# Eight matmuls of ones behind the transpose of the negated maxima, and key heads 376 elements apart

## The chip, the cores and the metric

One Trainium2 chip, one of its cores. The metric is the device time of one execution in microseconds (us), the median over several runs.

## What is computed

Two transformer layers on a batch of 8, with 112 tokens of width 256 per batch and a context of 375 tokens:

```python
x = x + L0_xcond(layernorm(x), ctx, ctx, tau, delta)   # 16 heads of 16, keys and values from ctx
x = x + L0_ffn(layernorm(x))                           # int8-like and ternary matmuls, conv of 3 taps, silu
x = x + L1_xcond(ctx, layernorm(x), len, pt)           # windowed attention
x = x + L1_ffn(layernorm(x))                           # 8 experts, one per token

# L0_xcond, the part that the change touches
scores = einsum('bhqd,bhkd->bhqk', q, k) * tau + delta
p_attn = softmax(scores / sqrt(DK), axis=-1)
x      = einsum('bhqk,bhkd->bhqd', p_attn, v)
```

## The kernel before

The work of the first three parts is a pipeline over the 8 batches. In one round of the loop at the end of the TensorE program, L874, the scores of one batch, the rest of the attention of the batch before, and the feed-forward and second attention of older batches are issued in an order written out by hand. The other engines have such loops too (SyncE, ScalarE, GpSimd, VectorE), and semaphores tie them together. A steady round takes some 31 us. After the rounds comes the expert layer.

Steps of the attention in `L0_xcond`, for batch b:

- `p_k`, `p_q`, `p_v` project keys, queries and values. Keys and queries are each split into three bf16 parts by ScalarE and GpSimd. SyncE writes the parts to DRAM (`p_kwrite` L475, `p_qwrite` L497) and reads them back (`p_kread` L478 to 489, `p_qread` L507) into the stacked tiles `kst` and `qst`. Partitions 0 to 95 of `kst` hold the parts of the keys in six bands of 16 partitions, 96 to 98 the bias `delta`, 99 to 101 ones. Each half of the heads (m = 0, 1) is read by three DMAs of 48, 32 and 16 partitions and a small one for `delta`.
- `a_scores(b, i)`, L694, computes two heads' scores, 112 queries by 375 keys. It reads `kst` as the moving operand, one head of even and one of odd number. VectorE takes the maxima (`a_max`, L1714), and `a_neg` negates them and splits them into three bf16 parts `nm`.
- TensorE's `a_max(b)`, L710, transposes `nm` into `pOb`. VectorE copies that to `nmT` (L1733), and ScalarE's queue issues three small DMAs (`a_stack`, L1179) that lay `nmT` into partitions 99 to 101 of `qst` and count up `nm_loaded`.
- `a_scoresT(b, n)`, L718, n = 0 to 11, computes the transposed scores, four heads and 125 keys at a time, with `kst` as the weights. The rows of `nmT` subtract the maximum. The result goes in turn to the two PSUM banks `pE[0]` and `pE[1]`, and ScalarE takes the exponential (`a_exp`, L1188, semaphore `exp_done`). `a_pv` multiplies with the values.

Between `a_max` and the first `a_scoresT` of a batch TensorE has `t_dg2` (L803, two records of a small fp32 matmul for the feed-forward; VectorE's `t_hq` L1611 scales with its result) and `p_v(i, 0)` (L653, whose result ScalarE copies to `vaug` before it goes on to the key split `p_km`). Behind the first two `a_scoresT` come `t_down` (L809), a third, `p_v(i, 1)`, a fourth, and `t_xqT` (L771), which waits for the quantized activations `xq` and the diagonal `dg` of VectorE (`t_xq`, L1614).

```python
def spin(n):
    for _ in range(n):
        mm(pS[:, 1, :], onesb[:, :], onesb[:, :].unsqueeze(1).to_broadcast([128, 4, 128]), True, True)
...
pe.wait_ge(ones_made, 1)
spin(8)
```

These eight matmuls of ones, 128x512 in bf16, stand at the start of TensorE's program already.

Of the kernel before, what the change touches and what calls it, by code (L numbers as in the profile page):

```python
# [5 lines left out]
def pixart_block(nc, A, out):  # L6
# [8 lines left out]
    B, T, D = A["x"].shape  # L15
    L = A["ctxT"].shape[3]
    NH, DK = 16, 16
    KT = 3
    LT = L // KT
    DC = D // 128  # L20
    HM = NH // DC
    HG = 4
    NG = NH // HG
    NP = NH // 2
    F0 = A["w1T"].shape[1] // DC
    M0 = F0 // 128
    NE, _, F1 = A["L1_ffn_W1"].shape
    M1 = F1 // 128
    FB = D
# [8 lines left out]
    KD = KS + 3  # L38
    KX = KD + 3
# [7 lines left out]
    with ctx:  # L47
        def sb(name, shape, dt=fp32):
            return ctx.enter_context(nc.sbuf_tensor(name, shape, dt))

        def sem(name):
            return ctx.enter_context(nc.semaphore(name))

        def dram(name, shape, dt=fp32):
            return nc.dram_tensor(name, shape, dt).ap()


        d_k = [dram(f"d_k{i}", [DC, 3, 128, L], bf16) for i in range(2)]
        d_q = [dram(f"d_q{i}", [DC, 3, 128, T], bf16) for i in range(2)]
        d_delta = dram("d_delta", [B, 3, L], bf16)  # L60
# [6 lines left out]

        EW = DC * F1 + M1 * D
        W = sb("W", [128, NE, EW])
# [4 lines left out]
        def carve(words):  # L74
            a = taken[0]
            taken[0] += words
            assert taken[0] <= (NE - 1) * EW
            return late[:, a:a + words]

        kst32 = [carve(NH * L // 2) for _ in range(2)]  # L80
        qst32 = [carve(NH * T // 2) for _ in range(2)]
        kst = [t.bitcast(bf16).rearrange("p (h l) -> p h l", h=NH) for t in kst32]
        qst = [t.bitcast(bf16).rearrange("p (h t) -> p h t", h=NH) for t in qst32]
        pexp = [carve(KT * HG * T).rearrange("p (k n) -> p k n", k=KT) for _ in range(2)]
        vaug = [carve(KT * NH * 32).rearrange("p (k h c) -> p k h c", k=KT, h=NH) for _ in range(2)]
        kf = carve(DC * L).rearrange("p (m l) -> p m l", m=DC)
        kr = carve(DC * L).rearrange("p (m l) -> p m l", m=DC)
# [37 lines left out]
        onesb = sb("onesb", [128, 128], bf16)  # L125
# [130 lines left out]
        pS = ps[:, 0:2, :]  # L256
        pE = [ps[:, 2, :], ps[:, 3, :]]
# [33 lines left out]
        exp_done = sem("exp_done")  # L291
# [19 lines left out]
        kst_loaded = [sem(f"kst_loaded{i}") for i in range(4)]  # L311
# [18 lines left out]
        ones_loaded = sem("ones_loaded")  # L330
# [103 lines left out]
        def _(sp):  # L434
# [42 lines left out]
            @batch  # L477
            def p_kread(b, m):  # L478

                sp.wait_ge(k_written[m], 16 * (b + 1))  # L480
                if b == 0:
                    sp.wait_ge(delta_written, 16)
                if b >= 2:
                    sp.wait_ge(st_ps, 12 * (b - 2) + 6 * (m + 1))
                src = d_k[b % 2][m].rearrange("t (d h) l -> (t d) (h l)", h=HM)
                dst = kst[b % 2][:, HM * m:HM * m + HM, :]
                for lo, n in ((0, 3), (48, 2), (80, 1)):
                    sp.dma_start(dst[lo:lo + 16 * n].rearrange("p h l -> p (h l)"), src[0:16 * n]).then_inc(kst_loaded[2 * m + b % 2], 16)
                sp.dma_start(dst[KS:KD], d_delta[b].unsqueeze(1).to_broadcast([3, HM, L])).then_inc(kst_loaded[2 * m + b % 2], 16)

            @batch
# [7 lines left out]
            @batch  # L499
            def p_qread(b):  # L500

                sp.wait_ge(q_written, 16 * (b + 1))
                if b >= 2:
                    sp.wait_ge(st_ps, 12 * (b - 1))
                src = d_q[b % 2].rearrange("m t (d h) l -> (t d) m (h l)", h=HM)
                for r, (tq, _) in enumerate(TERMS):
                    sp.dma_start(qst[b % 2][16 * r:16 * r + 16].rearrange("p (m h) l -> p m (h l)", m=DC),  # L507
                                 src[16 * tq:16 * tq + 16]).then_inc(qst_loaded[b % 2], 16)
# [36 lines left out]
            sp.dma_start(prepi[:, 0:1], A["_lenS2"].unsqueeze(1)).then_inc(len_loaded, 16)  # L545
            for i in range(2):
                sp.dma_start(qst32[i][KS:KD], A["ones"][:, 0:NH * T // 2]).then_inc(ones_loaded, 16)
                sp.dma_start(kst32[i][KD:KX], A["ones"][:, 0:NH * L // 2]).then_inc(ones_loaded, 16)
            sp.dma_start(ebn, A["L1_ffn_b2"]).then_inc(eb_loaded, 16)
            load_rows(1)  # L550
            load_ctx(1)
            for i in range(B + 5):
                w_delta(i - 2)
                w_win(i - 1)
                p_kwrite(i - 2, 0)
                p_ge(i - 2)
                w_tab(i - 2)
                p_qwrite(i - 2)
                p_kread(i - 2, 0)
                p_qread(i - 2)  # L560
                p_kwrite(i - 2, 1)
                p_ctx(i)
                p_kread(i - 2, 1)
                p_rows(i)
                w_eb(i - 5)
# [12 lines left out]
        def _(pe):  # L578
            def mm(o, l, r, start, stop):
                return pe.matmul(o, lhsT=l, rhs=r, start=start, stop=stop, skip_group_check=True)  # L580

            def tr(o, i, ident):
                n = i.shape[0]
                return pe.transpose(o, i, ident[0:n, 0:n])  # L584
# [68 lines left out]
            def p_v(b, half):  # L653
# [9 lines left out]
                for n, t in enumerate(((0, 1), (2,))[half]):  # L663
                    for k in range(DC):
                        last = mm(pY[0:LT, D * n:D * n + D], cxT[b % 2][:, k, LT * t:LT * t + LT], WvT[:, k, :], k == 0, k == DC - 1)
                last.then_inc(v_ps, 1)
# [26 lines left out]
            @batch  # L693
            def a_scores(b, i):  # L694

                if i == 0:
                    if b == 0:
                        pe.wait_ge(ones_loaded, 64)
                    pe.wait_ge(kst_loaded[b % 2], 64 * (b // 2 + 1))
                    pe.wait_ge(qst_loaded[b % 2], 96 * (b // 2 + 1))  # L700
                if i == NP // 2:
                    pe.wait_ge(kst_loaded[2 + b % 2], 64 * (b // 2 + 1))
                if b >= 1 or i >= 1:
                    pe.wait_ge(mx_done, NP * b + i)
                for n in range(2):
                    last = mm(pS[0:T, n, 0:L], qst[b % 2][0:KD, 2 * i + n, :], kst[b % 2][0:KD, 2 * i + n, :], True, True)
                last.then_inc(s_ps, 1)

            @batch
            def a_max(b):  # L710

                pe.wait_ge(nm_ready, b + 1)
                if b >= 1:
                    pe.wait_ge(o_evac, b)
                tr(pOb[0:3 * NH, 0:T], nm[:, :, :].rearrange("p t h -> p (t h)"), idb).then_inc(nmT_ps, 1)

            @batch
            def a_scoresT(b, n):  # L718
# [6 lines left out]
                for j in range(HG):  # L725
                    last = mm(pE[n % 2][0:LT, T * j:T * j + T], kst[b % 2][0:KX, HG * g + j, LT * t:LT * t + LT],
                              qst[b % 2][0:KX, HG * g + j, :], True, True)
# [3 lines left out]
            def a_pv(b, g):  # L731
# [5 lines left out]
                for t in range(KT):  # L737
                    for j in range(HG):
                        last = mm(pO[32 * j:32 * j + 32, T * g:T * g + T], vaug[b % 2][0:LT, t, HG * g + j, :],
                                  pexp[g % 2][0:LT, t, T * j:T * j + T], t == 0, t == KT - 1)  # L740
                last.then_inc(pv_ps, 1)
# [131 lines left out]

            for i in range(B + 6):  # L874
                a_scores(i - 1, 1)
                a_scoresT(i - 2, 6)
                u_xn2T(i - 4)
                p_G(i - 2)
                t_h(i - 3, 1)
                a_scores(i - 1, 2)  # L880
                a_scoresT(i - 2, 7)
                u_sc(i - 4)
# [47 lines left out]
            for b in range(B - 1):  # L930
                n = B - 1 - b
                mm(pY[0:T, (b + 1) * NE:B * NE], onesb[0:T, 0:T], ohb[:, b:b + 1, :].to_broadcast([T, n, NE]), False, n == 1)
            for b in range(B):
                last = mm(pY[:, B * NE:B * NE + NE], onesb[0:T, :], ohb[:, b, :], b == 0, b == B - 1)
            last.then_inc(route_ps, 1)
            pe.wait_ge(routed, LANES)
            for b in range(B):
                last = mm(pZ[:, 0:2 * NB], inlane[:, b, :], pair[:, b, :, :].rearrange("t c j -> t (c j)"), b == 0, b == B - 1)
# [40 lines left out]
            for b in range(B):  # L979
                last = mm(pZ[:, 64:64 + 3 * NB], inlane[:, b, :], share[:, b, :, :].rearrange("t c j -> t (c j)"), b == 0, b == B - 1)  # L980
# [17 lines left out]
        def _(act):  # L998
            def copy(dst, src):
                return act.activation(dst, src, ACT.Copy)  # L1000
# [123 lines left out]
            def p_v(b, half):  # L1124
# [6 lines left out]
                for n, t in enumerate(((0, 1), (2,))[half]):  # L1131
                    last = copy(vaug[b % 2][0:LT, t, :, 0:DK], pY[0:LT, D * n:D * n + D].rearrange("p (h c) -> p h c", c=DK))
                last.then_inc(v_evac, 1)
# [48 lines left out]
            def a_exp(b, n):  # L1182
# [3 lines left out]
                if b >= 1 or g >= 2:  # L1186
                    act.wait_ge(pv_ps, NG * b + g - 1)
                act.activation(pexp[g % 2][0:LT, t, :], pE[n % 2][0:LT, 0:HG * T], ACT.Exp).then_inc(exp_done, 1)  # L1188

# [882 lines left out]
```

## Time and profile before

| | us |
|---|---|
| median of 3 runs | 443.85 (442.79 to 444.97) |
| profiled execution, its own time | 443.59 |
| its span on the core | 441.7 |
| TensorE busy | 339.7 (77%) |
| VectorE busy | 251.7 (57%) |
| ScalarE busy | 202.9 (46%) |
| mean granted TensorE clock | 0.84 of full |

The profile lists, for each engine, what ran, how long, and how long the engine had been idle before it, with what ended the idle time. The chain of waits follows the end of the program back from release to release. The granted clock of TensorE is given as a share of 2.4 GHz, 1.00 or 0.50 in a stretch. PE is TensorE's matmuls, PEld its weight loads, DVE VectorE, ACT ScalarE, POOL GpSimd, SP SyncE; a trailing q marks the queue that issues DMAs. An fp32 matmul shows as several records.

### The profile page before, as it was taken

To read this page: it belongs to the slowest core of one execution; us is meant where nothing else is said; L and a number is where in the kernel's file an instruction comes from. 1 tells how busy PE (TensorE), PEld (TensorE's weight loads), DVE (VectorE), ACT (ScalarE), POOL (GpSimd) and SP (SyncE) were. 2 spreads that over 40 slices of the span, in tenths; PEclk is the share of its full clock that TensorE was granted. 3 is DMA by queue.
4 is the path that set the end of the run, shared out by engine and by line. 5 is a ranking of instruction groups with operands and counts; after the bars stand their busy time and mean duration, and the time that the engine had idled before them with its cause. 6 is when DMAs were issued, how large, how long until landed. Compare 5 with 4: busy or idle time off the path is not lost.

```text
span 441.7 us, 8239 instructions
## 1 busy us (share of the span) xinstructions
PE 339.7 (77%) x2713; PEld 262.7 (59%) x2713; DVE 251.7 (57%) x561; ACT 202.9 (46%) x543; POOL 197.1 (45%) x244
## 2 busy tenths in 40 slices
PE   6638498694996996995986868955451699999993
PEld 2415375573865865864856647542331598989982
DVE  3264346779589698787897884474417432322320
ACT  2402565595693783874964738233120233242320
POOL 3631503695375564745844917246131213232422
PEclk9566789899798897998998989565555599999999
DMA  8781654616417427637367112897720302111121
GB/s 255 286 206 29 141 133 85 153 37 156 115 31 144 100 41 150 180 88 174 83 123 194 28 32 88 301 381 241 245 79 3 95 0 66 28 59 49 31 62 37
DMA packets 36695, 52.24 MB, mean 118 GB/s; under 512 B 10495, under 2 KB 28744, under 8 KB 36390
## 3 DMA queue, kind: packets, MB, share of 16 engines
q1 hardware_dynamic: 27948, 34.69, 31.5%
q10 hardware_dynamic: 7056, 12.41, 9.0%
q0 software_dynamic: 1648, 4.59, 3.5%
q8 instruction: 23, 0.38, 0.4%
q14 instruction: 20, 0.16, 0.1%
HBM read 42.81 MB, written 9.31 MB: 118 GB/s over the span
## 4 chain that ended last, share of the span: by engine, by line
PE 54%; DMA 13%; DVE 11%; POOL 8%; issue 7%; ACT 3%; ACTq 2%; SPq 2%; DVEq 0%; POOLq 0%
PE ps L580 50%; DMA W<-nmT 7%; PE ps L584 4%; DMA d_q<-hold 2%; DVE hold L1611 2%; ACTq L1179 2%; POOL W L1479 2%; POOL W L1470 2%; POOL W L1487 2%; DMA W<-d_delta 1%; DMA prepi<-in__lenS 1%; SPq L507 1%; ACT hold L1000 1%; DVE mx L1714 1%; DMA out_x<-hold 1%
## 5 line engine op out<-in xcount | busy, mean ns | idle before, releaser
L580 PE MATMUL ps<-W 125*32 125x112 f32 (+2 forms) x1280 | 90.9, 267 | 43.0 <-DMA W<-nmT 30.8
L580 PEld LDWEIGHTS ps<-W 125*32 125x32 f32 (+2 forms) x1280 | 68.1, 127 | 65.7 <-DMA W<-nmT 34.1
L1714 DVE TENSOR_REDUCE mx<-ps 112x2 f32<-112x750 f32 x64 | 59.9, 936 | 38.9 <-PE ps L580 38.1
L1188 ACT ACTIVATE W<-ps 125x448 f32<-125x448 f32 x96 | 50.8, 542 | 39.2 <-PE ps L580 38.8
L580 PE MATMUL ps<-hold,proj 128*128 128x128 f32 (+2 forms) x288 | 55.9, 343 | 3.1 <-ACT W L1107 2.0
L1362 ACT ACTIVATE hold<-ps,consts 128x128 f32<-128x128 f32 x88 | 25.0, 370 | 50.2 <-PE ps L580 50.2
L580 PEld LDWEIGHTS ps<-hold,proj 128*128 128x128 f32 x288 | 40.1, 201 | 12.5 <-issue 3.8
L584 PE MATMUL ps<-consts,hold 112*128 112x112 f32 (+3 forms) x136 | 28.8, 303 | 22.8 <-DMA hold<-d_x,hold 5.6
L1591 POOL DMA_INDIRECT out_x<-hold x11 | 16.3, 1479 | 62.5 <-DVE hold L1992 60.0
L580 PE MATMUL ps<-hold 128*128 128x128 f32 (+4 forms) x256 | 37.4, 299 | 8.5 <-DVE hold L1611 5.8
L580 PE MATMUL ps<-proj,hold 128*125 128x256 f32 (+1 forms) x128 | 41.7, 468 | 1.1 <-ACT hold L1082 1.0
L580 PE MATMUL ps<-W,hold 128*128 x176 | 40.9, 386 | 0.0
L580 PEld LDWEIGHTS ps<-hold 128*128 128x128 f32 (+3 forms) x256 | 32.1, 201 | 11.1 <-DVE hold L1611 6.3
L584 PEld LDWEIGHTS ps<-consts,hold 112*128 112x128 f32 (+3 forms) x136 | 16.5, 150 | 35.8 <-issue 9.1
L580 PEld LDWEIGHTS ps<-W,hold 128*128 128x128 f32 x176 | 32.5, 190 | 5.3
L1495 POOL TENSOR_TENSOR rstd<-ve,expo 112x1 f32<-112x1 f32 x24 | 15.8, 658 | 43.0 <-DVE ve L1614 43.0
L1000 ACT ACTIVATE hold<-ps 128x224 f32<-128x224 f32 (+5 forms) x72 | 24.5, 352 | 22.3 <-PE ps L580 13.0
L580 PEld LDWEIGHTS ps<-proj,hold 128*125 128x125 f32 (+1 forms) x128 | 27.9, 235 | 6.2 <-issue 1.2
L1409 POOL TENSOR_TENSOR W<-W 128x375 f32<-128x375 f32 x16 | 14.7, 917 | 35.4 <-ACT W L1000 35.4
L1000 ACT ACTIVATE W<-W 128x375 bf16<-128x375 f32 x32 | 16.5, 516 | 23.4 <-issue 20.5
L1992 DVE SCALAR_TENSOR_TENSOR hold<-ps,hold 128x256 f32<-128x256 f32 x11 | 5.3, 484 | 38.4 <-PE ps L580 38.4
L1223 ACT ACTIVATE W<-W,consts 128x112 f32<-128x112 f32 x64 | 25.3, 472 | 0.2
(167 smaller groups left out, 574.0 us busy)
## 6 DMA issues: line engine op xcount, KB each, us to landing
W<-in_L_ffn_W SPq DMA_DIRECT2D x10, 1024.0 KB, 11.4
W<-in_L_ffn_W ACTq DMA_DIRECT2D x6, 1024.0 KB, 6.8
d_k<-W SPq DMA_DIRECT2D x16, 281.2 KB, 3.5
W<-d_k SPq DMA_DIRECT2D x16, 281.2 KB
hold<-in_ctxT SPq DMA_DIRECT2D x8, 375.0 KB, 3.8
W<-d_k SPq DMA_DIRECT2D x16, 187.5 KB
W<-d_q SPq DMA_DIRECT2D x48, 56.0 KB, 3.2
d_x<-hold ACTq DMA_DIRECT2D x8, 224.0 KB, 2.6
```

The source lines that it names most:

```text
L580: return pe.matmul(o, lhsT=l, rhs=r, start=start, stop=stop, skip_group_check=True)
L584: return pe.transpose(o, i, ident[0:n, 0:n])
L1000: return act.activation(dst, src, ACT.Copy)
L1179: act.dma_start(qst[b % 2][KD + t:KD + t + 1], nmT[16 * t:16 * t + 16, :]).then_inc(nm_loaded[b % 2], 16)
L1188: act.activation(pexp[g % 2][0:LT, t, :], pE[n % 2][0:LT, 0:HG * T], ACT.Exp).then_inc(exp_done, 1)
L1223: last = act.activation(yc[:, m, :], hs[:, m, 1:1 + T], ACT.Identity, bias=cb[:, m:m + 1], scale=cw[:, m, 1:2])
L1362: act.activation(hxT[:, j % 2, f, :], ps[:, 2 * (j % 2) + f // 4, 128 * (f % 4):128 * (f % 4) + 128], ACT.Gelu, bias=b1T[:, bass.ds(e * M1 ...
L1409: pool.tensor_tensor(kr[:, m, :], kf[:, m, :], kt3[:, m, 0, :], ALU.subtract).then_inc(kr_made, 1)
L1470: pool.tensor_tensor(right, hs[:, ms, 2:2 + T], cw[:, ms, 2:3].to_broadcast([128, M0 // 2, T]), ALU.mult)\
L1495: step(pool.tensor_tensor(rstd[:, which, s], ve[:, which:which + 1], expo[0:T, :], ALU.pow))
L1591: pool.indirect_dma_start(out.rearrange("b t d -> (b t) d"), bass.IndirectOffsetOnAxis(ap=outi[:, j:j + 1], axis=0), ysb[:, j % 2, :], Non ...
L1714: dve.tensor_reduce(mx[:, 2 * i:2 * i + 2], pS[0:T, :, 0:L], X, ALU.max).then_inc(mx_done, 1)
```

## The change

`kst` gets 376 instead of 375 elements per head. The reads from DRAM and the matmuls leave the last element of each head out, so that a read that wrote 8 heads of a partition as one run of 3000 elements now writes 8 runs of 375. The tile of ones that fills the last partitions is 3008 words long instead of 3000. On TensorE, `a_max` is followed by a wait for all exponentials of the batch before (from the second batch on) and eight 128x512 bf16 matmuls of ones into `pE[1]`, which nothing reads.

```diff
+    LP = L + 1
...
-        kst32 = [carve(NH * L // 2) for _ in range(2)]
+        kst32 = [carve(NH * LP // 2) for _ in range(2)]
...
-                src = d_k[b % 2][m].rearrange("t (d h) l -> (t d) (h l)", h=HM)
-                dst = kst[b % 2][:, HM * m:HM * m + HM, :]
+                src = d_k[b % 2][m].rearrange("t (d h) l -> (t d) h l", h=HM)
+                dst = kst[b % 2][:, HM * m:HM * m + HM, 0:L]
                 for lo, n in ((0, 3), (48, 2), (80, 1)):
-                    sp.dma_start(dst[lo:lo + 16 * n].rearrange("p h l -> p (h l)"), src[0:16 * n]).then_inc(kst_loaded[2 * m + b % 2], 16)
+                    sp.dma_start(dst[lo:lo + 16 * n], src[0:16 * n]).then_inc(kst_loaded[2 * m + b % 2], 16)
...
-                sp.dma_start(kst32[i][KD:KX], A["ones"][:, 0:NH * L // 2]).then_inc(ones_loaded, 16)
+                sp.dma_start(kst32[i][KD:KX], A["ones"]).then_inc(ones_loaded, 16)
...
-                    last = mm(pS[0:T, n, 0:L], qst[b % 2][0:KD, 2 * i + n, :], kst[b % 2][0:KD, 2 * i + n, :], True, True)
+                    last = mm(pS[0:T, n, 0:L], qst[b % 2][0:KD, 2 * i + n, :], kst[b % 2][0:KD, 2 * i + n, 0:L], True, True)
...
                 tr(pOb[0:3 * NH, 0:T], nm[:, :, :].rearrange("p t h -> p (t h)"), idb).then_inc(nmT_ps, 1)
+                if b >= 1:
+                    pe.wait_ge(exp_done, KT * NG * b)
+                for _ in range(8):
+                    mm(pE[1], onesb[:, :], onesb[:, :].unsqueeze(1).to_broadcast([128, 4, 128]), True, True)
...
-    laid["ones"] = _np.full((3, 3000), 0x3F803F80, _np.uint32).view(_np.float32)
+    laid["ones"] = _np.full((3, 3008), 0x3F803F80, _np.uint32).view(_np.float32)
```

On TensorE, the place around `a_max` in a steady round before (`idb,nm` is the transpose, `W,onesf` `t_dg2`, `proj,hold` `p_v`, `W 125x112` `a_scoresT`):

```order
L584 MATMUL ps<-idb,nm 48x112 [waits o_evac,nm_ready]
L580 MATMUL ps<-W,onesf 128x112 [waits dg2_ready]
L580 MATMUL ps<-proj,hold 125x256 [waits V2_made,q_evac]
L580 MATMUL ps<-proj,hold 125x256 x3
L580 MATMUL ps<-W 125x112 [waits exp_done,nm_loaded1]
L580 MATMUL ps<-W 125x112 x3
```

The same place with the change:

```order
L585 MATMUL ps<-idb,nm 48x112 [waits o_evac,nm_ready]
L581 MATMUL ps<-onesb 128x512 [waits exp_done]
L581 MATMUL ps<-onesb 128x512 x7
L581 MATMUL ps<-W,onesf 128x112 [waits dg2_ready]
L581 MATMUL ps<-proj,hold 125x256 [waits V2_made,q_evac]
L581 MATMUL ps<-proj,hold 125x256 x3
L581 MATMUL ps<-W 125x112 [waits exp_done,nm_loaded1]
L581 MATMUL ps<-W 125x112 x3
```

Nothing else moved on TensorE: `t_dg2` and `p_v` now stand behind the eight new matmuls.

On SyncE's queue, the read of half the keys before (48, 32 and 16 partitions, `delta`, then the queries):

```order
L488 DMA W<-d_k 48x3000 [waits st_ps,k_written0]
L488 DMA W<-d_k 32x3000
L488 DMA W<-d_k 16x3000
L489 DMA W<-d_delta 3x8x375
L507 DMA W<-d_q 16x2x896 [waits st_ps,q_written]
```

and with the change:

```order
L489 DMA W<-d_k 48x8x375 [waits st_ps,k_written0]
L489 DMA W<-d_k 32x8x375
L489 DMA W<-d_k 16x8x375
L490 DMA W<-d_delta 3x8x375
L508 DMA W<-d_q 16x2x896 [waits st_ps,q_written]
```

The order is the same. The 96 runs of 6000 bytes of each half became 768 runs of 750.

## Rows read from the trace of the kernel before

**Rows 1.** The page, part 4: the chain that ended last, by line.
```profile
PE ps L580 50%; DMA W<-nmT 7%; PE ps L584 4%; DMA d_q<-hold 2%; DVE hold L1611 2%; ACTq L1179 2%; POOL W L1479 2%; POOL W L1470 2%; POOL W L1487 2%; DMA W<-d_delta 1%; DMA prepi<-in__lenS 1%; SPq L507 1%; ACT hold L1000 1%; DVE mx L1714 1%; DMA out_x<-hold 1%
```

**Rows 2.** Waits of TensorE: engine, line, awaited; us in total, times, longest.
```profile
PE ps L580 <- DMA W<-nmT: 30.8, 8, 4.6
```

**Rows 3.** Timeline of TensorE, six batches' first `a_scoresT`: start, us, idle before.
```profile
53.25 0.67 PE L580 MATMUL ps<-W 102*125 102x112 bf16 x8 [3.21 <-DMA W<-nmT]
...
80.53 0.67 PE L580 MATMUL ps<-W 102*125 102x112 bf16 x8 [4.40 <-DMA W<-nmT]
...
140.84 1.10 PE L580 MATMUL ps<-W 102*125 102x112 bf16 x8 [3.38 <-DMA W<-nmT]
...
172.23 1.10 PE L580 MATMUL ps<-W 102*125 102x112 bf16 x8 [4.02 <-DMA W<-nmT]
...
204.23 0.99 PE L580 MATMUL ps<-W 102*125 102x112 bf16 x8 [4.64 <-DMA W<-nmT]
...
262.15 0.89 PE L580 MATMUL ps<-W 102*125 102x112 bf16 x8 [2.76 <-DMA W<-nmT]
```

**Rows 4.** Timeline of all engines, 130 to 144 us: before and behind that wait.
```profile
135.25 0.47 PE L580 MATMUL ps<-W,onesf 112*128 112x112 f32 x2
...
135.46 1.81 ACTq L1179 DMA_DIRECT2D W<-nmT  x3
...
135.56 1.90 PE L580 MATMUL ps<-proj,hold 128*125 128x256 f32 x8
...
136.54 1.08 DVE L1611 TENSOR_TENSOR W<-W,ps 128x896 f32<-128x896 f32 x1
...
138.25 0.64 ACT L1000 ACTIVATE W<-ps 125x256 f32<-125x256 f32 x2
...
141.74 1.92 PE L580 MATMUL ps<-w2T,W 128*112 128x256 bf16 x8
...
143.33 0.27 DVE L1614 TENSOR_SCALAR W<-consts,tiny 112x112 f32<-112x112 f32 x1
```

**Rows 5.** Timeline of TensorE, 138 to 172 us, the same batch further on.
```profile
143.86 2.03 PE L580 MATMUL ps<-proj,hold 128*125 128x256 f32 x4
...
146.09 0.39 PE L584 MATMUL ps<-idb,hold 112*128 112x112 bf16 x2
```

**Rows 6.** Stretches at half clock: length, busy of each engine, PEclk, DMA share, GB/s.
```profile
109.00:115.60 6.60, 5.51 (x31) 5.03 (x31) 3.45 (x9) 1.92 (x5) 2.53 (x5) 0.50 0.24 67
139.60:146.40 6.80, 5.56 (x31) 5.07 (x32) 5.30 (x11) 1.97 (x5) 4.02 (x7) 0.50 0.22 64
170.40:177.00 6.60, 4.77 (x24) 4.36 (x25) 5.26 (x11) 1.52 (x3) 3.20 (x4) 0.50 0.63 124
...
262.50:265.80 3.30, 3.30 (x25) 3.30 (x24) 2.60 (x10) 1.58 (x4) 0.00 (x0) 0.50 0.48 97
```

**Rows 7.** Timeline of TensorE, windows one matmul apart: an even head, then both.
```profile
148.62 0.33 PE L580 MATMUL ps<-W 99*112 99x375 bf16 x1
...
148.62 0.49 PE L580 MATMUL ps<-W 99*112 99x375 bf16 x2
```

**Rows 8.** Timeline of TensorE: the matmuls of ones at the start; a shorter idle stretch.
```profile
1.40 3.59 PE L580 MATMUL ps<-onesb 128*128 128x512 bf16 x8 [1.40 <-POOL hold L1381]
...
101.06 0.41 PE L584 MATMUL ps<-consts,hold 112*128 112x112 f32 x2 [1.67 <-DVE hold L1611]
```

**Rows 9.** Stretches as in rows 6: `p_kwrite` alone, then `p_kread` alone.
```profile
142.00:143.10 1.10, 1.10 (x7) 1.10 (x6) 1.05 (x2) 0.53 (x2) 0.69 (x1) 0.50 0.81 262
149.10:150.60 1.50, 1.50 (x24) 1.50 (x21) 1.50 (x3) 1.23 (x4) 1.01 (x2) 1.00 0.92 224
```

**Rows 10.** The page, part 6: DMA issues, KB each, us from issue to landing.
```profile
d_k<-W SPq DMA_DIRECT2D x16, 281.2 KB, 3.5
...
d_q<-hold SPq DMA_DIRECT2D x8, 168.0 KB, 4.0
```

**Rows 11.** Timeline of all engines, the last batch's three small DMAs.
```profile
259.12 1.82 ACTq L1179 DMA_DIRECT2D W<-nmT  x3
```

## The prediction

> **What bounds the kernel now.** I read the chain of waits first. Half of the span is TensorE, and the largest single thing in it that is no engine is the landing of the small DMAs of `nmT`, 7% [rows 1]. TensorE waits for it once per batch, 8 times, 30.8 us in all [rows 2]. The timeline shows each wait: 3.21, 4.40, 3.38, 4.02, 4.64 and 2.76 us for batches 0, 1, 3, 4, 5 and 7 [rows 3], and the two left out, batches 2 and 6, share the rest of the 30.8, 8.4, so 4.2 each. The clock comes next. Behind these waits TensorE ran at the lower of its two levels, 1.2 GHz: 5.51, 5.56 and 4.77 us of busy time at 0.50 for batches 2, 3 and 4, and 3.30 for batch 7, which stands for batches 1, 5 and 6 too [rows 6]. That is 5.51 + 5.56 + 4.77 + 4 x 3.30 = 29.0 us of work at half speed, on the path. The same eight `a_scoresT` matmuls take 0.67 us where the clock had not yet fallen and 1.10 where it had [rows 3]. So a round loses time twice: in the wait, and in the slow stretch that it causes.
>
> **The ones, their own cost.** In a pair of score matmuls the second ends 0.49 - 0.33 = 0.16 us after the first [rows 7], so 375 columns pass in 0.16 us at full clock, which is 2.4 GHz. Eight times 512 columns then take 4096 / 375 x 0.16 = 1.75 us. The upper bound is 3.59 us, what the same eight took at the start, with the tail of the last in it [rows 8]. I take 1.75, since TensorE works without a gap in front of `a_max` in a steady round. They stand ahead of `t_dg2` and `p_v`, and these were done 3.38 us before the DMA landed in the tightest steady round [rows 3], so all of the 1.75 lies in the wait: cost 0. At 3.59 they would overrun it by 0.2 in batch 3 and by 0.8 in batch 7, 1 us in all. The wait for `exp_done` that goes with them costs nothing, because `a_pv` of the last group of that batch has already waited for the same count, 12 per batch, earlier in the round.
>
> **What is late behind them.** `nmT` itself is not: the transpose stands ahead of the ones. `t_dg2` ran at 135.25 to 135.72, and VectorE took its result at 136.54 [rows 4]. It now ends 1.75 later, at 137.47, so VectorE's `t_hq` starts 0.93 us later, and with it the rest of its queue, up to the diagonal `dg` that ended at 143.60 and that `t_xqT` needs [rows 4]. TensorE came to `t_xqT` at 146.09 [rows 5], 2.5 us of cover. That cover goes when TensorE gets faster. ScalarE's copy of `p_v`, 138.25 to 138.89, also moves by 1.75 us, to 140.6, still ahead of the first exponential, which needs the matmuls of 140.84.
>
> **What a kept clock gives.** For a round like batch 3, from 140.84 to `t_xqT`: the first eight matmuls save 1.10 - 0.67 = 0.43 [rows 3], `t_down` half of 1.92 = 0.96 [rows 4], `p_v(i, 1)` half of 2.03 = 1.0 [rows 5], and two further groups of `a_scoresT` 0.2 each, by the same ratio. Sum 2.8. The exponentials between the groups do not get faster; I take off 0.4. That brings `t_xqT` to 143.7, against a `dg` at 143.6 plus 0 to 0.93 of lateness; I take 0.5 in the middle. Left: 1.9 us. Batch 2 the same, batch 4 1.7. For batches 1, 5, 6 and 7, with 3.3 instead of 5.5 us at half clock, 2.4 x 3.3 / 5.5 - 0.5 = 0.95 each. All held would be 1.9 + 1.9 + 1.7 + 4 x 0.95 = 9.3 us. In ScalarE's and VectorE's busy part of the round behind it everything only moves forward.
>
> **Is it kept?** The idle time left is the wait less 1.75: for batches 0 to 7 1.5, 2.65, 2.45, 1.6, 2.3, 2.9, 2.45 and 1.0 us. An idle stretch of 1.67 us inside a round left the clock at full [rows 8]; the waits of 2.76 us and more of batches 1 to 7 were each followed by a fall [rows 3, 6]. So batches 3 and 7 should hold, 1.9 + 0.95 = 2.85 us. Five lie between the two rows; I count half of 1.9 + 1.7 + 3 x 0.95 = 6.45, so 3.2. Together 6.1 us.
>
> **The padding.** For the matmuls it gives nothing: the odd head, which now starts 2 bytes off a word, passed its 375 columns at full pace already [rows 7]. It can cost in the reads. A half is 562 KB, in flight when `nmT` is on its way; one run in 6000 bytes becomes eight of 750. The nearest row with runs of 750 bytes is `p_kwrite`, the other direction: 262 GB/s at a DMA share of 0.81, while `p_kread` gets 224 at 0.92 [rows 9]. By that rate the read is not slower, and could be 0.3 us quicker. The other end: `p_qwrite`, 768 runs and 168 KB, lands in 4.0 us, `p_kwrite`, 384 runs and 281 KB, in 3.5 [rows 10]. The 384 further runs cost 0.5 and the 113 KB fewer, 0.43 at 262 GB/s; 0.93 in all, which makes 1.6 us for the 672 further runs of a half. I take 0.2, near the row with the same size of run, 8 x 0.2 = 1.6 us for the eight landings of `nmT`. The second half's read shows in no wait of TensorE above a microsecond, and stays off the path.
>
> The Trainium skill, page "DMA: Bandwidth & Descriptors", section "Why small descriptors are slow", gives a fixed overhead of some 3 cycles per packet besides one for each 32 bytes. An estimate from that page is 8 x (24 + 3) = 216 cycles against 188 + 3 = 191, 13% or 0.3 us of a half's 2.5, so 2.4 instead of 1.6 us in the sum. No run here shows it.
>
> **Sum.** 443.59 of the profiled execution - 6.1 + 1.6 = 439.1. The median lies 0.26 above that execution: **439.3 us**.
>
> **Rivals.** *All seven hold* (0.16): idle stretches up to 2.9 us are survived. 443.85 - 9.3 + 1.6 = 436.2. For it, nothing stood between 1.67 and 2.76; against, 2.76 was not survived by batch 7.
>
> *Shorter runs let `nmT` through* (0.10). In the last batch, with no read in flight, TensorE went on 3.0 us after the first issue (259.12 to 262.15); in batch 3 it was 5.4 (135.46 to 140.84) [rows 3, 4, 11]. The small DMAs lose 2.4 us to the big reads. If they no longer queue behind whole runs of 6000 bytes, half of it, 1.2 us in seven batches, makes 8.4, and all clocks hold: 443.85 - 9.3 - 8.4 = 426.1. The Trainium skill, page "DMA: Bandwidth & Descriptors", section "Queues, rings and completion order", says that an engine switches between queues only at packet boundaries, a packet being several descriptors. By that rule eight short runs may form one packet as before, which is why I give this little.
>
> *The ones do not do their work* (0.20): whatever idle time is left is enough for the fall, except in batches 3 and 7. 443.85 - 2.85 + 1.6 = 442.6, no change.
>
> *The reads get longer and take `nmT` with them* (0.18), the other side. Place: `p_kread` of the first half, issued just ahead of the small DMAs. Price: 1.2 us a batch, toward the end of 1.6 above, with no clock held, since the idle stretches grow by as much: 443.85 + 8 x 1.2 = 453.4; the bound is 443.85 + 12.8 = 456.7. It decides from 6.1 / 8 = 0.76 us per batch. For it, the DMA engines are near full there (0.92) and 8 times the runs go through one queue; against, the rate of rows 9.
>
> My forecast, half of the open five, has the rest, 0.36.
>
> **Chances.** About 0.5% (2.2 us) can be told from no change: 441.6 to 446.1. Faster: 0.32 of the forecast's 0.36, 0.16, 0.10, and 0.03 of the third rival: 0.61. The same: 0.04 + 0.17 + 0.03 = 0.24. Slower: 0.15. The range takes in the forecast, the all-held and the no-effect cases with their bounds, reaches down to the edge of the second rival, 427, and up into the fourth, 450.
>
> **What would show it.** In the profile of the changed kernel: eight `onesb` matmuls behind each `idb,nm` in 1.75 us; TensorE's wait for `nmT` at 16.8 us in all instead of 30.8; 1.00 behind it in batches 3 and 7 and in some others; 0.67 for the first eight matmuls there; a wait of `t_xqT` for VectorE of up to a microsecond in held rounds; the time from issue to landing of `nmT` unchanged within 0.3 us. It is wrong if that wait stays above 25 us (reads longer), if it nearly vanishes (small DMAs let through), or if the clock falls in every round.

## The result and the profile after

| | before | with the change |
|---|---|---|
| median | 443.79 us (5 runs, 438.73 to 444.97) | 446.86 us (5 runs, 443.88 to 447.83) |
| ratio | | 1.0123, 95% interval 1.0075 to 1.0170 |
| profiled execution | 443.59 us | 443.88 us, the quickest of its five |
| span | 441.7 us | 442.2 us |
| TensorE busy | 339.7 us | 346.5 us |

The change makes the kernel slower by 1.2%. 439.3 us and faster was forecast. The ratio and its interval are taken over the fast runs; the two medians stand 3.1 us, 0.7%, apart.

The chain of waits after, by line (answers to rows 1):

```profile
PE ps L581 49%; DMA W<-nmT 6%; PE ps L585 4%; POOL W L1484 2%; DVE hold L1616 2%; POOL W L1492 2%; POOL W L1475 2%; ACTq L1184 2%; DVE hold L1619 1%; DVE mx L1719 1%; DVE W L1616 1%; DMA W<-d_delta 1%; DVE W L1619 1%; DMA prepi<-in__lenS 1%; DMA d_q<-hold 1%
```

TensorE's waits after: us in total, times, longest (rows 2):

```profile
PE ps L581 <- DMA W<-nmT: 20.2, 8, 3.8
...
PE ps L581 <- DMA W<-d_q: 5.9, 1, 5.9
...
PE ps L581 <- DMA W<-d_delta: 1.1, 1, 1.1
```

The wait for `nmT` fell from 30.8 to 20.2 us, by 10.6. The ones take more than that: some 1.75 us in each of batches 1 to 7, and 3.6 in batch 0, where they ran at half clock. From the transpose `idb,nm` to the first `a_scoresT`, summed over the eight batches, it is 53.3 us where it was 49.7. So the landings came later by 3.6 us in sum, 0.45 per batch, as TensorE sees it. The small DMAs themselves, KB each and median us from issue to landing, before and then after:

```profile
W<-nmT ACTq DMA_DIRECT2D x24, 3.5 KB, 4.6
```

```profile
W<-nmT ACTq DMA_DIRECT2D x24, 3.5 KB, 5.1
```

TensorE's timeline after, around batch 3 and at the first `a_scoresT` of batches 1, 4, 5 and 7 (rows 3 and 5):

```profile
81.45 0.67 PE L581 MATMUL ps<-W 102*125 102x112 bf16 x8 [3.17 <-DMA W<-nmT]
...
136.61 1.90 PE L581 MATMUL ps<-onesb 128*128 128x512 bf16 x8
138.35 0.37 PE L581 MATMUL ps<-W,onesf 112*128 112x112 f32 x2
138.56 1.90 PE L581 MATMUL ps<-proj,hold 128*125 128x256 f32 x8
143.36 0.67 PE L581 MATMUL ps<-W 102*125 102x112 bf16 x8 [2.90 <-DMA W<-nmT]
...
147.78 0.26 PE L585 MATMUL ps<-idb,hold 112*128 112x112 bf16 x2
...
174.39 0.84 PE L581 MATMUL ps<-W 102*125 102x112 bf16 x8 [3.15 <-DMA W<-nmT]
...
206.40 1.10 PE L581 MATMUL ps<-W 102*125 102x112 bf16 x8 [3.81 <-DMA W<-nmT]
...
265.64 0.67 PE L581 MATMUL ps<-W 102*125 102x112 bf16 x8 [1.27 <-DMA W<-nmT]
```

The ones take what was reckoned: `t_dg2` starts 1.74 us behind the first of them. But batch 3 still waits 2.90 us, where 1.6 was foreseen. From the first small DMA's issue at 136.96 to 143.36 it is 6.40 us, against 5.38 before [rows 3, 4].

Stretches behind these waits: length, busy of each engine, PEclk, DMA share, GB/s (rows 6):

```profile
113.40:116.60 3.20, 3.20 (x15) 2.91 (x14) 2.21 (x7) 1.18 (x3) 0.42 (x2) 0.50 0.22 67
144.10:147.30 3.20, 3.20 (x16) 2.91 (x15) 2.60 (x9) 1.26 (x3) 0.29 (x1) 0.50 0.21 63
174.80:178.10 3.30, 3.30 (x19) 3.12 (x18) 2.26 (x7) 1.52 (x3) 0.36 (x1) 0.50 0.65 133
205.50:212.20 6.70, 5.80 (x32) 5.31 (x33) 3.57 (x9) 2.21 (x5) 2.38 (x4) 0.50 0.69 222
...
263.50:266.80 3.30, 2.03 (x19) 1.61 (x17) 2.56 (x6) 0.69 (x2) 1.15 (x2) 1.00 0.02 3
```

The clock held in batch 7, and in batch 0, whose wait was down to 0.5 us; it fell in batches 1 to 6. In 2, 3 and 4 it fell later than before and for a shorter time, 3.2 to 3.3 instead of 4.8 to 5.6 us of work; in batch 5 it was the other way, 5.80 instead of 3.3. In the held batch 7 `t_xqT` waited for VectorE, as the prediction had said of held rounds:

```profile
268.53 0.27 PE L585 MATMUL ps<-idb,hold 112*128 112x112 bf16 x2 [0.78 <-DVE W L1619]
```

The read of the keys (rows 9), a stretch with little beside it (`nmT` and the first queries), and the queue that issues it (three DMAs, 1.88 us in all):

```profile
137.30:139.60 2.30, 2.30 (x13) 1.69 (x12) 1.59 (x4) 0.53 (x2) 0.67 (x2) 1.00 1.08 169
```

```profile
135.71 1.88 SPq L489 DMA_DIRECT2D W<-d_k  x3
```

It moves 169 GB/s at a DMA share of 1.08, where it moved 224 at 0.92. The same stretch of the first half's read before, 135.7 to 138.0, has 220 at 0.94. An estimate from the rates 169 and 224 is that a half of 562 KB takes 3.3 instead of 2.5 us.

### The profile page after: what moved, and what is told of

It is laid out like the page before. It is cut to its first block, busy times and chain, and to the rows that moved or that the text cites. A ratio compares the mean times of both kernels' runs of the same rounds, so it can differ in the third digit from the quotient of the medians.

```text
span 442.2 us, 8367 instructions
## 1 busy us (share of the span) xinstructions
PE 346.5 (78%) x2777; PEld 263.8 (60%) x2777; DVE 248.5 (56%) x561; ACT 202.8 (46%) x543; POOL 198.0 (45%) x244
## 4 chain that ended last, share of the span: by engine, by line
PE 53%; DVE 14%; DMA 10%; POOL 8%; issue 7%; ACT 3%; ACTq 2%; SPq 1%; DVEq 0%; POOLq 0%
PE ps L581 49%; DMA W<-nmT 6%; PE ps L585 4%; POOL W L1484 2%; DVE hold L1616 2%; POOL W L1492 2%; POOL W L1475 2%; ACTq L1184 2%; DVE hold L1619 1%; DVE mx L1719 1%; DVE W L1616 1%; DMA W<-d_delta 1%; DVE W L1619 1%; DMA prepi<-in__lenS 1%; DMA d_q<-hold 1%
## 5 line engine op out<-in xcount | busy, mean ns | idle before, releaser
L581 PE MATMUL ps<-W 125*32 125x112 f32 (+2 forms) x1280 | 90.8, 272 | 34.6 <-DMA W<-nmT 20.2
L581 PE MATMUL ps<-hold,proj 128*128 128x128 f32 (+2 forms) x288 | 53.6, 334 | 3.6 <-ACT W L1112 2.2
L581 PEld LDWEIGHTS ps<-hold,proj 128*128 128x128 f32 x288 | 39.0, 197 | 11.6 <-ACT W L1112 3.3
L1500 POOL TENSOR_TENSOR rstd<-ve,expo 112x1 f32<-112x1 f32 x24 | 14.8, 616 | 41.3 <-DVE ve L1619 41.3
L1005 ACT ACTIVATE W<-W 128x375 bf16<-128x375 f32 x32 | 16.5, 516 | 24.5 <-issue 22.1
```

Of the source, the lines that this page charges most:

```text
L1500: step(pool.tensor_tensor(rstd[:, which, s], ve[:, which:which + 1], expo[0:T, :], ALU.pow))
```

## The experiments

All were timed against the kernel before, in three series: the first four experiments (442.48 us before), the next four (441.18) and the last four (442.15). Ratios are to the kernel before of the same series, with 95% intervals.

### The padding alone

```diff
-                if b >= 1:
-                    pe.wait_ge(exp_done, KT * NG * b)
-                for _ in range(8):
-                    mm(pE[1], onesb[:, :], ...)
```
(against the change)

> Only the padding of the key tile, without the matmuls of ones. Theory R (the 750-byte runs lengthen the read of the keys and with it the landing of nmT, by 0.4 to 1.0 us a batch in the profile after): slower than before by 4 to 8 us, time from the first small DMA's issue to the first a_scoresT up by 0.4 to 1.0 us in most batches. Theory O (the padding costs nothing, the ones push t_dg2, p_v and what hangs on them back): within 1 us of before.

Measured: 449.69 us against 442.48, ratio 1.0165 (1.0117 to 1.0214). That is 7.3 us, inside theory R's 4 to 8. TensorE's wait for `nmT`, and its single wait for queries, before the first scores:

```profile
PE ps L581 <- DMA W<-nmT: 33.0, 8, 4.9
...
PE ps L581 <- DMA W<-d_q: 6.0, 1, 6.0
```

The second was 4.8 us before and is 6.0 with the ones alone too, so it is not put down to the padding. The waits for `nmT` account for 2.2 us (33.0 - 30.8). From the transpose to the first `a_scoresT` the sum is 52.2 us against 49.7: 2.5 us, 0.3 per batch, and 0.4 or more in four of the eight.

The span of this profiled execution is 448.0 us against 441.7, so 3.8 of 6.3 us lie elsewhere. Nearly all of it, 3.5, lies between a first `a_scoresT` and the next transpose: 2.4 behind batches 0 and 1 and 3.0 behind batch 6, less 1.9 behind the four between them. Behind batch 6 TensorE worked at half clock from 255.3 to 261.3, where it had run at full. The same 26 score matmuls before, then here:

```profile
251.03 1.24 PE L580 MATMUL ps<-W 99*112 99x375 bf16 x26 [0.28 <-DVE mx L1714]
```

```profile
255.35 2.15 PE L581 MATMUL ps<-W 99*112 99x375 bf16 x26
```

It is not shown that the padding causes this fall: the padded long runs without ones, below, take as long in that place (26.1 us, here 26.4, before 23.4).

The mean clock from 70 to 265 us fits a loss through the clock. Before, then here:

```profile
70.00:265.00 195.00, 159.98 (x1563) 122.97 (x1561) 156.03 (x330) 124.92 (x330) 114.48 (x135) 0.91 0.48 108
```

```profile
70.00:265.00 195.00, 162.09 (x1563) 123.15 (x1555) 151.37 (x316) 125.35 (x329) 113.79 (x134) 0.89 0.54 108
```

0.02 of 195 us at a level that is half of full is 0.02 x 195 / 0.5 = 7.8 us more at half clock, at most 3.9 us of lost time; the two shares are rounded to a hundredth, so this is a rough figure. The same bytes, 108 GB/s, now keep the DMA engines busy for 0.54 instead of 0.48.

### The ones alone

```diff
                 tr(pOb[0:3 * NH, 0:T], ...).then_inc(nmT_ps, 1)
+                if b >= 1:
+                    pe.wait_ge(exp_done, KT * NG * b)
+                for _ in range(8):
+                    mm(pE[1], onesb[:, :], ...)
```
(against the kernel before)

> Only the eight matmuls of ones behind the transpose, the key tile as before. Theory R: faster than before by 3 to 6 us, idle time before the first a_scoresT some 1.75 us less, one slow stretch of 3.4 instead of 6.8 us in batches 2 to 4. Theory O: slower than before by 2 to 5 us.

Measured: 440.19 us, ratio 0.9928 (0.9893 to 0.9964), 3.2 us faster by the ratio and 2.3 by the medians. The ones do help, at the lower end of what theory R gave them. The two halves multiply to 1.0165 x 0.9928 = 1.009, within the interval of the whole change. The wait for `nmT` and batch 3 here:

```profile
PE ps L580 <- DMA W<-nmT: 16.5, 8, 3.2
```

```profile
139.97 0.67 PE L580 MATMUL ps<-W 102*125 102x112 bf16 x8 [1.81 <-DMA W<-nmT]
```

```profile
140.10:143.30 3.20, 3.20 (x23) 3.01 (x23) 3.10 (x6) 1.52 (x3) 2.06 (x2) 0.65 0.32 97
```

16.5 us is the 16.8 of the forecast. But 1.81 us of idle time in batch 3 did not hold the clock: 0.65 over the stretch behind it. It held in batches 0 and 7, behind 0.20 and 1.26 us, and fell in 1 to 6.

### Padded, but in long runs again, with the ones

```diff
-        d_k = [dram(f"d_k{i}", [DC, 3, 128, L], bf16) for i in range(2)]
+        d_k = [dram(f"d_k{i}", [DC, 3, 128, LP], bf16) for i in range(2)]
...
-        kt3 = carve(3 * DC * L // 2).bitcast(bf16).rearrange("p (m t l) -> p m t l", t=3, m=DC)
+        kt3w = carve(3 * DC * LP // 2).bitcast(bf16).rearrange("p (m t l) -> p m t l", t=3, m=DC)
+        kt3 = kt3w[:, :, :, 0:L]
...
-                sp.dma_start(dst[lo:lo + 16 * n], src[0:16 * n])...
+                sp.dma_start(dst[lo:lo + 16 * n].rearrange("p h l -> p (h l)"), src[0:16 * n])...
```
(against the change; `src` is again `(t d) (h l)`, `dst` all 376 elements, `p_kwrite` writes `kt3w`, and GpSimd fills its last column with zeros once)

> The key tile padded and the ones kept, but the copy in DRAM and the source tile padded as well, so that each partition is read as one run of 6016 bytes again. Theory R (run length): as fast as the ones alone, 3 to 6 us below before. If the padded addresses themselves were the cost: as slow as the change, 3 us above before. Theory O: also 3 us above before.

Measured: 436.45 us, ratio 0.9759 (0.9687 to 0.9831). The padded addresses are no cost; with one run per partition the change would have made the kernel faster, by 2.4% by the ratio and by 1.4% by the medians. The size is uncertain: the six runs spread from 429.25 to 439.75 us.

### The ones behind `p_v`

```diff
                 p_v(i, 0)
+                a_ones(i - 1, 8)
                 a_scoresT(i - 1, 0)
```
(against the kernel before; `a_ones` holds the wait and the ones)

> The key tile as before, and the eight matmuls of ones behind p_v(i, 0), right ahead of the first a_scoresT, so that t_dg2 and p_v are not pushed back. Theory R: 4 to 8 us below before, somewhat better than the ones right behind the transpose, since VectorE gets t_dg2 as early as before. Theory O: equal to before or faster, and clearly faster than the ones behind the transpose.

Measured: 438.86 us, ratio 0.9857 (0.9801 to 0.9913). Better than 0.9928 behind the transpose, but the intervals overlap, so this alone does not show that the place matters.

### Padded in long runs, without the ones

> The key tile padded, source tile and DRAM copy padded too, so each partition is read as one run of 6016 bytes, and no matmuls of ones. The run length theory: within 2 us of before, and 5 to 9 us below the padding with short runs. If padded rows are quicker to move, as the 4 us between the long runs with ones and the ones alone suggest: 2 to 5 us below before.

The kernel of the long runs above less its ones. Measured: 438.77 us, ratio 0.9946 (0.9901 to 0.9992). Just faster than before, and far below the short runs. One of its batches kept the clock with no ones at all:

```profile
138.92 0.67 PE L582 MATMUL ps<-W 102*125 102x112 bf16 x8 [3.25 <-DMA W<-nmT]
```

```profile
138.90:142.20 3.30, 3.25 (x32) 2.96 (x33) 3.19 (x6) 2.08 (x5) 2.00 (x2) 1.00 0.29 90
```

3.25 us idle, survived at 1.00; 1.81 us above was not. The length of the idle stretch alone does not decide.

### Short runs, the key tile not padded

```diff
-        d_k = [dram(f"d_k{i}", [DC, 3, 128, L], bf16) for i in range(2)]
+        d_k = [dram(f"d_k{i}", [DC, 3, 128, LP], bf16) for i in range(2)]
...
-                sp.dma_start(d_k[b % 2][m].rearrange("t p l -> p t l"), kt3[:, m])...
+                sp.dma_start(d_k[b % 2][m].rearrange("t p l -> p t l")[:, :, 0:L], kt3[:, m])...
...
-                src = d_k[b % 2][m].rearrange("t (d h) l -> (t d) (h l)", h=HM)
+                src = d_k[b % 2][m].rearrange("t (d h) l -> (t d) h l", h=HM)[:, :, 0:L]
```
(against the kernel before; `dst` is given as partition, head, element)

> The key tile as before at 375 elements a head, without the ones; only the copy in DRAM is padded, so that the read is 768 runs of 750 bytes a half instead of 96 of 6000. The run length theory: as slow as the padding alone, 5 to 9 us above before. If the padded tile's addresses were the cost: within 1 us of before.

Measured: 450.86 us, ratio 1.0229 (1.0170 to 1.0289). All of the slowdown, with the tile left as it was: it is the 768 runs instead of 96. The copy in DRAM is padded here, but it is in the padded long runs too, and those are not slow. The issue of the DMAs, min, median and max ns of one, here and then with padded long runs:

```profile
L489 SPq DMA_DIRECT2D W<-d_k x48: 562/610/1584, 20.8 to 242.2; - x48
```

```profile
L490 SPq DMA_DIRECT2D W<-d_k x48: 312/418/1959, 20.7 to 232.1; - x48
```

By the medians issuing one takes 610 instead of 418 ns (416 before), so the next DMA in the queue is later by 0.2 us for each, 0.6 per half.

### Long runs, ones behind `p_v`: eight, then sixteen

> Padded with long runs, and eight matmuls of ones behind p_v(i, 0) instead of behind the transpose. If pushing back t_dg2 and p_v costs: 1 to 4 us below the same with the ones behind the transpose. If the place is indifferent: equal within 1 us.

> As the run before with sixteen matmuls of ones, 3.5 us, which nearly fill the wait for nmT. If the clock is what the ones work through, it stays at full in all batches from 2 on and the time falls by 2 to 5 us against eight; where the ones overrun the landing (last batch by 1 us) that is lost again. If the ones only cost time: slower than eight by 3 us or more.

Measured: eight 432.90 us, ratio 0.9812 (0.9757 to 0.9867); sixteen 429.97 us, ratio 0.9754 (0.9706 to 0.9801), the quickest kernel of this study. The waits of TensorE with sixteen:

```profile
PE ps L582 <- DMA W<-nmT: 2.7, 4, 1.2
```

Against the eight behind the transpose, 0.9759, the eight here are no faster by the ratio, while the medians, 432.90 of 441.18 against 436.45 of 442.48, say the reverse. With eight, the runs do not settle whether the place matters. The expectation of another 2 to 5 us from eight to sixteen held for the medians, 2.9, within overlapping intervals. With sixteen the clock stayed at full behind the waits of batches 2 to 7, as expected; in batch 1 it fell behind a wait of 1.19 us.

### Sixteen ones behind `p_v`, key tile as before

> The key tile as before, sixteen matmuls of ones behind p_v(i, 0). If the held clock is worth what the sixteen showed on the padded long runs: 2 to 5 us below eight at the same place, so 435 to 438 against a before of 442. If only the long padded runs made it work: equal to eight within 1 us.

Measured: 432.43 us, ratio 0.9784 (0.9732 to 0.9835). Eight at the same place had 438.86 and 0.9857: 6.4 us between the medians of the two series, 3.2 us between the ratios, whose intervals still overlap a little. The kernel is called e9_late16 in the next expectation. The fall behind the wait is gone in all eight batches. Batch 3 and a stretch behind the wait of batch 5:

```profile
133.10 3.62 PE L580 MATMUL ps<-onesb 128*128 128x512 bf16 x16
136.84 0.67 PE L580 MATMUL ps<-W 102*125 102x112 bf16 x8
137.34 1.04 PE L580 MATMUL ps<-w2T,W 128*112 128x256 bf16 x8
138.22 0.39 PE L580 MATMUL ps<-W 102*125 102x112 bf16 x4
138.44 1.09 PE L580 MATMUL ps<-proj,hold 128*125 128x256 f32 x4
139.37 0.39 PE L580 MATMUL ps<-W 102*125 102x112 bf16 x4
139.59 0.26 PE L584 MATMUL ps<-idb,hold 112*128 112x112 bf16 x2
```

```profile
196.90:200.30 3.40, 3.40 (x37) 3.24 (x38) 3.23 (x7) 2.22 (x5) 1.35 (x1) 1.00 0.61 126
```

From the first `a_scoresT` to `t_xqT` it is 2.75 us, where it was 146.09 - 140.84 = 5.25 [rows 3, 5]: 2.5 us is what a held clock gives in batch 3, close to the 2.4 of the forecast before the lateness of VectorE.

### The same sixteen, short runs with the padded tile

> The padding of the change with its short runs, and sixteen matmuls of ones behind p_v(i, 0). If the cost of the short runs works mostly through the clock (longer waits, more falls), the held clock takes most of it back: within 2 us of e9_late16. If it works through the landing itself: 5 to 9 us above e9_late16.

Measured: 440.00 us, ratio 0.9965 (0.9928 to 1.0003). 1.0185 of the kernel before it, 8 us, the size of the padding alone, with the clock held behind the waits of batches 2 to 7 in both. So here most of the cost of the short runs is not in the clock, and half of it is in the landings of `nmT`:

```profile
PE ps L581 <- DMA W<-nmT: 7.8, 6, 2.0
PE ps L581 <- DMA W<-d_delta: 4.1, 4, 1.9
```

The longest wait for `nmT` in batches 2 to 7, and the stretch behind it:

```profile
203.00 0.67 PE L581 MATMUL ps<-W 102*125 102x112 bf16 x8 [1.55 <-DMA W<-nmT]
```

```profile
203.00:206.40 3.40, 3.40 (x37) 3.23 (x38) 2.51 (x9) 2.20 (x5) 0.28 (x2) 1.00 0.60 124
```

With the tile and its runs as before, the wait for `nmT` is 3.7 us and that for `W<-d_delta` 4.0. The first four of the 8 us stand there. Another 1.6 lies in the round behind batch 1, where the clock fell behind a wait of 2.04 us and had held behind 0.93. Two more lie ahead of the first transpose, at 47.50 instead of 45.49; but that start is at 46.64 before and at 46.73 with the padding alone, so these two are not shown to be the padding's.

### Twelve ones; and sixteen right behind the transpose

> Padded long runs with twelve matmuls of ones behind p_v(i, 0), 2.6 us. Between eight (0.981 of before) and sixteen (0.975): 0.978. If the clock needs the idle time under some 2 us in every batch, twelve are enough and the ratio is that of sixteen or a little better, since the last batch is overrun less.

> Padded long runs with sixteen matmuls of ones right behind the transpose, where the change has its eight. If pushing t_dg2 and p_v back by 3.5 us costs: 2 to 5 us above the same sixteen behind p_v. If the place is indifferent: equal within 1 us.

Measured: twelve 431.50 us, ratio 0.9767 (0.9720 to 0.9815), the same as sixteen. Sixteen behind the transpose 443.55 us, ratio 1.0054 (1.0016 to 1.0093): 0.030 above the same sixteen behind `p_v`, so 13 us lost by the place alone, far more than the 2 to 5 expected. TensorE's timeline there:

```profile
133.99 3.63 PE L582 MATMUL ps<-onesb 128*128 128x512 bf16 x16
137.45 0.37 PE L582 MATMUL ps<-W,onesf 112*128 112x112 f32 x2
...
143.70 0.27 PE L586 MATMUL ps<-idb,hold 112*128 112x112 bf16 x2 [0.89 <-DVE W L1621]
```

`t_dg2` is late, so VectorE's `t_hq` and `t_xq` are, and `t_xqT` waits 0.89 us for them. It waits so in batches 2, 3, 4 and 7, 3.5 us in all, and in no batch with the sixteen behind `p_v`. The rest of the 13 us is not placed, and late `p_v` was not tried apart from late `t_dg2`.

## Why the prediction was wrong

**The step that failed is the term for the padding's cost.** The text took 0.2 us per batch, 1.6 in all, "near the row with the same size of run". The padding alone measured 7.3 us, and 10 us with the tile unpadded. Two things were off. The landings of `nmT`, the only path that the term priced, came later by 0.3 us per batch with the padding alone, by 0.45 with the change and by 0.5 with the tile unpadded, 2.5, 3.6 and 3.8 in sum instead of 1.6. And the cost outside of these landings was put at nothing: with the padding alone it is 3.8 of the 6.3 us between the profiled executions. Part of that is work at half clock in other places, as in the round behind batch 6; how much of it the padding causes stays open, and so does the rest.

The row that the 0.2 rested on was `p_kwrite`, which writes DRAM: 750 bytes a run at 262 GB/s. The read of the same runs the other way gets 169. A row with the right size of run and the wrong direction was taken for the nearest. It has half as many runs too, over 128 instead of 96 partitions, and no run separates that from the direction.

Of the rivals, "the reads get longer and take `nmT` with them", given 0.18, named the place and the side. Its price of 1.2 us a batch is over twice what the landings show, and they stay under its point of decision, 0.76, as well; the whole cost of the padding, 7.3 / 8 = 0.9, does not. "Shorter runs let `nmT` through" was wrong: from issue to landing the small DMAs took 5.1 us instead of 4.6.

The estimate from the Trainium skill, page "DMA: Bandwidth & Descriptors", section "Why small descriptors are slow", 13% more for a half, was too small as well: the rates above, 224 and 169 GB/s, make it 33%, and 30% from the 220 of the first half.

**What the padding was said not to give** is open to a doubt of another kind. For the matmuls it gave nothing, as said. Padded in long runs it is faster than before by 0.5%, just outside of no difference, and with the eight ones added it beats the ones alone by 1.7% by the ratios (0.9759 against 0.9928) and 0.8% by the medians (436.45 against 440.19). Source, DRAM copy and tile all changed there, and the runs became 6016 and 752 bytes; which of it helps was not tried.

**The ones' own cost** was right but for batch 0, where they ran at half clock and took 3.6 us: 1.75 us, hidden in the wait, 16.5 us of idle time left against 16.8 said. Their wait for `exp_done` showed nowhere.

**What a kept clock gives** was right in size where it was kept: 2.5 us in batch 3. **Is it kept** was wrong: 1.81 us of idle time in batch 3 of the ones alone did not hold it, and none of the five others held behind its wait; of the seven batches that were counted 7 alone did, with the ones alone and in the change. (Of the five that "lie between the two rows", batch 5 with its 2.9 us lay above both.) Instead the falls of batches 2 to 4 became shorter, 3.3 instead of up to 5.6 us of work. Batch 0 was left out of the sum: its clock fell before and held with the ones. The text had reckoned with neither gain. Ones alone: 3.2 us against 6.1 said, the second term that was mis-sized.

**The lateness behind them** was named rightly, `t_dg2` to `t_hq` to `t_xq` to `t_xqT`. In the change it shows as the 0.78 us of batch 7. With eight ones the place shows no cost beyond the noise; with sixteen it is 13 us.

**"The second half's read stays off the path"** was right for the kernel with the change to a microsecond, and wrong for the better ones: once the clock holds, `W<-d_delta`, the last DMA of that half, is waited for 4.0 us with sixteen ones behind `p_v`, and the chain there has 4% of it instead of 1% [rows 1].

In sum, the forecast had - 6.1 + 1.6. Measured by the parts it is - 3.2 + 7.3 = + 4.1, and together + 5.4 by the ratio (0.0123 x 443.8) and + 3.1 by the medians. 446.86 lies inside the stated range of 427 to 450 us, on the side of it that was given 0.15.

## What to carry to other kernels

A padding that breaks one long run per partition into many is paid in the DMA, and in the transfers that land behind it; here, with the source and the copy padded too, the run stayed whole and the cost was gone. A DMA price is to be taken from a row of the same direction, not only of the same size of run, and the landing that it delays is not the whole price. Matmuls of ones that bridge a wait stood best right in front of the waiting instruction, behind all useful work, and enough of them to nearly fill it: twelve to sixteen here made 2.2 to 2.5%, and ahead of `t_dg2` and `p_v` the same sixteen gave all of it back.

## What was not expected of the hardware

The same 108 GB/s over the rounds cost a DMA share of 0.54 in runs of 750 bytes and 0.48 in runs of 6000, and issuing one of the DMAs took 610 ns instead of 418. An idle stretch of 3.25 us left TensorE's clock at full in one batch and one of 1.81 us took it down to 1.2 GHz in another, so the stretch's length is no safe measure. With 1.55 us or less it never fell behind the wait in batches 2 to 7 of the kernels with sixteen ones behind `p_v`; in batch 1 of one of them it fell behind 1.19 us.
